# A state-space layer and a mixture of experts on one core: VectorE in chunk 0's lead, expert rows fetched in 32x32 blocks, squares per row tile

## The reference

```python
# part 1: a selective state space layer (512 inner channels, 16 states)
xn = rms_norm(ln(x)) * norm_w
x_inner, gate = split(xn @ in_proj_w)             # 256 -> 2 x 512
x_inner = x_inner * silu(gate)
xc = causal_conv(x_inner, conv_w)                 # 4 taps per channel
dt = softplus(xc @ dt_w + dt_b); Bm = xc @ B_w; Cm = xc @ C_w
h = exp(dt * A) * h + dt * Bm * xc                # along time, per channel and state
y = sum over states (h * Cm) + D_skip * xc
x = x + ln(y @ out_proj_w)
# part 2: 8 experts, the best 2 per row, and one shared expert
t = ln(x); logits = t @ gate_w; p, i = softmax of the top 2
x = x + ln(sum over the 2 (p * ((silu(t @ Wg[i]) * (t @ Wu[i])) @ Wd[i]))
           + (silu(t @ Sg) * (t @ Su)) @ Sd)
```

## Time and profile before

| what | value |
|---|---|
| median of 3 runs | 1672.4 us (1670.68 to 1673.68) |
| the profiled execution, its own time | 1672.79 us |
| its span | 1671.2 us |
| mean granted TensorE clock | 0.961 of full |
| PE busy | 1490.7 us, 89% |
| DVE busy | 1329.3 us, 80% |
| POOL busy | 1037.5 us, 62% |
| ACT busy | 1026.2 us, 61% |

### The profile page before, as it was taken

One profiled execution on the slowest core, in us unless ns is written; L12 is line 12 of the kernel. 1 busy time (PEld: TensorE's weight loads), 2 busy tenths in 40 slices (PEclk: granted clock), 3 DMA queues, 4 the chain that ended last, 5 costly groups with the idle time before them and its releaser, 6 DMA issues.

```text
span 1671.2 us, 23917 instructions
## 1 busy us (share of the span) xinstructions
PE 1490.7 (89%) x6642; PEld 991.6 (59%) x6642; DVE 1329.3 (80%) x2297; ACT 1026.2 (61%) x2140; POOL 1037.5 (62%) x1183
## 2 busy tenths in 40 slices
PE   6788799999999999999998677798999999999990
PEld 3354555655655655656656555476777777777760
DVE  4399999999999899999899994276666666676765
ACT  3567678679678678688686665254445454454544
POOL 0678779889889899899799884322222222323224
PEclk9999899999999999999999879799999999999995
DMA  6111112211221221211213734314222222222226
GB/s 205 39 51 39 51 57 67 85 58 40 88 63 46 73 62 54 80 52 55 67 52 114 221 104 158 130 27 133 33 36 36 36 36 36 36 36 36 36 32 206
DMA packets 88031, 119.90 MB, mean 72 GB/s; under 512 B 11168, under 2 KB 62208, under 8 KB 87904
## 3 DMA queue, kind: packets, MB, share of 16 engines
q1 hardware_dynamic: 66976, 86.61, 16.8%
q0 software_dynamic: 16704, 27.57, 8.4%
q10 hardware_dynamic: 4224, 4.19, 0.7%
HBM read 84.72 MB, written 33.10 MB: 71 GB/s over the span
## 4 chain that ended last, share of the span: by engine, by line
PE 40%; DVE 10%; POOL 9%; issue 9%; ACT 5%; DMA 1%; DVEq 0%; POOLq 0%; ACTq 0%; SPq 0%
PE A L1272 11%; PE bA L1241 10%; PE bH L1241 10%; POOL arena L1032 6%; DVE arena L870 5%; DVE arena_t L887 2%; PE bH L603 2%; PE A L484 1%; ACT bA L766 1%; PE A L566 1%; PE A L1263 1%; PE A L533 1%; DMA sum_scratch<-arena_t 1%; PE A L474 1%; POOL expert_in_scratch L1020 1%
## 5 line engine op out<-in xcount | busy, mean ns | idle before, releaser
L1032 POOL TENSOR_TENSOR arena<-arena 128x512 f32<-128x512 f32 x512 | 644.8, 1275 | 96.8 <-DVE arena L870 95.7
L766 ACT ACTIVATE bA<-arena,a_neg 128x512 f32<-128x512 f32 x512 | 350.5, 690 | 192.5 <-DVE arena L870 191.2
L603 PEld LDWEIGHTS bH<-ident,arena 128*128 128x128 f32 x2048 | 248.8, 145 | 285.1 <-issue 123.3
L603 PE MATMUL bH<-ident,arena 128*128 128x128 f32 x2048 | 324.7, 285 | 70.9 <-DVE arena L870 53.6
L870 DVE TENSOR_TENSOR_SCAN arena<-bA,arena 128x512 f32<-128x512 f32 x256 | 305.4, 1210 | 49.0 <-ACT bA L766 32.4
L870 DVE TENSOR_TENSOR_SCAN arena<-bA,hl,arena 128x512 f32<-128x512 f32 x256 | 321.2, 1270 | 2.5 <-ACT bA L766 2.1
L1305 ACT COPY hT<-arena_t 32x160 f32<-32x160 f32 x568 | 182.5, 321 | 77.0 <-DVE arena_t L1289 71.2
L1295 DVE STREAM_TRANSPOSE hT<-arena_t 32x192 f32<-32x192 f32 x568 | 206.1, 363 | 6.6
L1400 POOL DMA_INDIRECT sum_scratch<-arena_t x71 | 113.6, 1599 | 148.4 <-issue 120.7
L1272 PE MATMUL A<-arena,hT 128*128 x852 | 198.4, 383 | 2.1 <-DVE hT L1295 2.1
L1394 POOL DMA_DIRECT2D arena_t<-expert_in_scratch x71 | 40.8, 575 | 256.7 <-issue 256.7
(11 more groups left out here) (194 smaller groups left out, 2019.9 us busy)
## 6 DMA issues: line engine op xcount, KB each, us to landing
arena<-b_scratch SPq DMA_DIRECT2D x128, 256.0 KB, 3.2
arena_t<-expert_in_scratch POOLq DMA_DIRECT2D x71, 132.0 KB, 2.4
arena<-in_L_ffn_Wg_dram SPq DMA_DIRECT2D x8, 704.0 KB, 5.8
arena<-in_L_ffn_Wu_dram SPq DMA_DIRECT2D x8, 704.0 KB, 7.4
arena<-in_L_ffn_Wd_dram SPq DMA_DIRECT2D x8, 640.0 KB, 8.3
arena_x<-in_L_attn_x_dram SPq DMA_DIRECT2D x9, 512.0 KB, 5.0
arena<-in_L_attn_x_dram SPq DMA_DIRECT2D x8, 512.0 KB, 5.0
x_scratch<-arena_x SPq DMA_DIRECT2D x8, 512.0 KB, 3.2
```

The lines of the kernel that those rows point to most:

```text
L603: i = e.transpose(bH[g % NH][:, q * P:(q + 1) * P], hh[:, (n - 1) % 2, q, d * P:(d + 1) * P], ident[:])
L766: e.activation(bA[g % NA][:], dt[c % 2][:, d, :], ACT.Exp, scale=a_neg[:, d, n:n + 1]).then_inc(s_a, 1)
L1032: e.tensor_tensor(bb[:, k % NB, :], u[c % 2][:, d, :], br[:, n % NR, :], ALU.mult).then_inc(s_bb, 1)
```

## The change

It has three parts.

**Chunk 0's lead.** The convolutions of channel tiles 2 and 3 of chunk 0 are done by VectorE as one multiplication and three multiply-adds each (`dve_convs`), ahead of the 28 statistics. VectorE also takes chunk 0's softplus sums and input products (`step_sum`, `step_input`) from GpSimd and the norm of chunk 1's rows (`dve_norm_x`) from ScalarE. The first three scans, the first four decays and the first four GpSimd products stand inside the lead, between the `dt` steps of the channel tiles, instead of behind all of them.

**Expert rows.** SyncE fetches tile t (`sp_fetch`): eight DMAs, each moving four 32x32 blocks to where the other side of the diagonal is, and one for the 8 extra columns into a buffer of its own (`xm`, 8 deep). VectorE then transposes within 32x32 blocks (`dve_turn_in`), straight into `xtT`. TensorE's two transposes and ScalarE's copy go. A row buffer is free when its tile has been turned; the wait for the store stands only at `xm` and at the result scatter. The load of `x1` stands behind the fetch of tile 12.

**Squares.** Each square waits for its own addition, not for all four.

```diff
+FIRST = (2, 3)
+def by_hand(name, c):
+    return c == 0 and name in [f"cv{d}" for d in FIRST]
...
 def pe_lead(e, k, c):
-                e.wait_ge(s_xn, J * (c + 1))
                 room(e, b, c)
                 for j in range(J):
+                    e.wait_ge(s_xn, J * c + (J if c else j + 1))
...
@@ act_proj
                 e.activation(dt[par][:, m, :], dt[par][:, m, :], ACT.Ln, bias=1.0).then_inc(s_ln, 1)
+                if c == 0 and m:
+                    act_decay(e, 0, m - 1)
+                if c == 0 and m == ND - 1:
+                    act_decay(e, 0, m)
...
@@ act_post
-        if k == ACT_AT["square_xf"]:
-            e.wait_ge(s_x1, J * (c + 1))
-            for j in range(J):
-                i = e.activation(xf[:, j, 0:DM], xr[:, j, :], ACT.Square, bias=mv[:, c * J + j, 0:1], accum_out=sqx[:, j:j + 1])
-            i.then_inc(s_cl, 1)
+        for j in range(J):
+            if k == ACT_AT["square_xf"][j]:
+                e.wait_ge(s_x1, J * c + j + 1)
+                e.activation(xf[:, j, 0:DM], xr[:, j, :], ACT.Square, bias=mv[:, c * J + j, 0:1], accum_out=sqx[:, j:j + 1]).then_inc(s_cl, 1)
...
+    def dve_norm_x(e):
+        e.wait_ge(s_p0n, 2)
+        e.wait_ge(s_x, 32)
+        all_filled(e, ["xnT0", "xnT1"], 0)
+        for j in range(J):
+            i = e.tensor_scalar(xn[:, j, :], xp[:, j, :], r0[:, J + j:J + j + 1], nmr[:, J + j:J + j + 1], ALU.mult, ALU.add)
+        i.then_inc(s_xn, J)
+
+    def dve_convs(e):
+        for d in FIRST:
+            emptied(e, f"inner{d}", 0)
+        for q in range(TAPS):
+            for i, d in enumerate(FIRST):
+                to, tap = xc[0][:, d, :], w_cv[:, d, q:q + 1]
+                if q == 0:
+                    e.tensor_scalar(to, xin[:, d, 0:CH], tap, None, ALU.mult).then_inc(s_cv, 1)
+                else:
+                    e.wait_ge(s_cv, len(FIRST) * (q - 1) + i + 1)
+                    e.scalar_tensor_tensor(out=to, in0=xin[:, d, q:q + CH], scalar=tap, in1=to, op0=ALU.mult, op1=ALU.add).then_inc(s_cv, 1)
...
@@ dve_scans
-                if (loop, k) == (-1, 26):
+                if (loop, k) == (-1, max(DVE_AT["inner"])):
+                    dve_convs(e)
                     dve_stats_x(e, 1)
+                for m in range(ND):
+                    if (loop, k) == (-1, POOL_AT["dt"][m]):
+                        step_sum(e, 0, m)
+                        step_input(e, 0, m)
+                        if m == 0:
+                            dve_norm_x(e)
+                        else:
+                            dve_scan(e, 0, m - 1)
...
+    def sp_fetch(e, t):
+        if t >= NX:
+            e.wait_ge(s_kx, t + 1 - NX)
+        row = e.value_load(tab[0:1, 1, t:t + 1], min_val=0, max_val=SPARE + (E - 1) * P)
+        for q in range(P // BLK):
+            for k in range(KD):
+                e.dma_start(xt[q * BLK:(q + 1) * BLK, t % NX, k * P:(k + 1) * P].rearrange("j (a i) -> j a i", i=BLK),
+                            xs_d[bass.ds(row, P), k * P + q * BLK:k * P + (q + 1) * BLK].rearrange("(a j) i -> j a i", j=BLK)).then_inc(s_in[t % NX], 16)
+        if t >= NM:
+            e.wait_ge(s_gt, t + 1 - NM)
+            e.wait_ge(s_ys, 16 * (t + 1 - NM))
+        e.dma_start(xm[:, t % NM, :], xs_d[bass.ds(row, P), DM:RW]).then_inc(s_in[t % NX], 16)
...
+    def dve_turn_in(e, t):
+        fetched(e, t)
+        if t >= 2:
+            e.wait_ge(s_gu, t - 1)
+        e.transpose(xtT[:, t % 2, :, :].rearrange("p k q -> p (k q)"), xt[:, t % NX, :]).then_inc(s_kx, 1)
...
@@ sync_tiles
+        for t in range(NT):
+            sp_fetch(e, t)
+            if t == E + NX:
+                e.wait_ge(s_x1s, 16 * NCH)
+                for u in range(NU):
+                    e.dma_start(x1s[:, u, :, :], unit_rows(x1_d, u)).then_inc(s_x1u, 16)
...
@@ pool_tiles
+        for t in range(NT):
+            fetched(e, t)
+            e.wait_ge(s_yt, t + 1)
+            if t:
+                e.wait_ge(s_ys, 16 * t)
+            e.indirect_dma_start(out=sh_d, out_offset=bass.IndirectOffsetOnAxis(ap=xm[:].bitcast(U32)[:, t % NM, TOK - DM:TOK - DM + 1], axis=0),
+                                 in_=yt[:, t % 2, :], in_offset=None, compute_op=ALU.add).then_inc(s_ys, 16)
...
@@ pe_tiles
-            if t + 1 < NT:
-                pe_turn_in(e, t + 1)
...
@@ dve_tiles
+            if t + 1 < NT:
+                dve_turn_in(e, t + 1)
```

More of the change, by code:

```diff
@@ L83, in bank_table @@
             for names, c, now in ((POST, loop - 2, SLOTS + k), (PROJ, loop + 1, k), (POST, loop - 1, k), (LEAD, loop + 2, k)):
-                turn += [(name, c) for name in names if 0 <= c < NCH and slot(names, name, c) == now]
+                turn += [(name, c) for name in names if 0 <= c < NCH and slot(names, name, c) == now and not by_hand(name, c)]
     return {use: (i % NQ, i // NQ + 1) for i, use in enumerate(turn)}
@@ L186, in program @@
     take = places(arena_t)
-    xt = take(NX, RW)
+    xt = take(NX, DM)
     xtT = take(2, KD, P)
@@ L191, in program @@
     yt = take(2, DM)
[L192 removed]
+    xm = take(NM, RW - DM)
+    ge, gn = (arena_t[:, o:o + (NT + 1) * E].rearrange("p (t e) -> p t e", e=E) for o in (NX * DM + 2 * KD * P, NX * DM + 2 * KD * P + (NT + 1) * E))
     arena_x = sb("arena_x", [P, NU * UT * DM])
@@ L343, in program, with convs_filled, convs_emptied @@
     GATES, INNERS, CONVS = ([f"{name}{d}" for d in range(ND)] for name in ("gate", "inner", "cv"))
+    def convs_filled(e, c):
+        all_filled(e, [name for name in CONVS if not by_hand(name, c)], c)
+        e.wait_ge(s_cv, TAPS * len(FIRST))
+    def convs_emptied(e, c):
+        all_emptied(e, [name for name in CONVS if not by_hand(name, c)], c)
+        e.wait_ge(s_cv, TAPS * len(FIRST))
     def sh(c):
@@ L478, in pe_proj @@
             for q in range(TAPS):
-                if k == PROJ[b] + THIRD[q]:
+                if k == PROJ[b] + THIRD[q] and not by_hand(b, c):
                     if q == 0:
@@ L632, in act_lead @@
         for j in range(J):
-            if k == ACT_AT["norm_x"][j]:
+            if k == ACT_AT["norm_x"][j] and c != 1:
                 if j == 0:
@@ L658, in act_proj @@
         for d in range(ND):
-            if k == ACT_AT["conv"][d]:
+            if k == ACT_AT["conv"][d] and not by_hand(f"cv{d}", c):
                 filled(e, f"cv{d}", c)
@@ L1102, in pool_scan @@
         for loop in range(-2, NCH + 2):
-            if loop == 0:
-                e.wait_ge(s_cst, 5)
-                for k in range(AHEAD_POOL):
-                    pool_input(e, 0, k)
             for k in range(SLOTS):
@@ L1132, in act_scan @@
                 e.wait_ge(s_an, 2)
-            if loop == 0:
-                for k in range(AHEAD_ACT):
-                    act_decay(e, 0, k)
             for k in range(SLOTS):
@@ L1192, in dve_scans @@
             for k in range(SLOTS):
-                if 0 <= loop < NCH:
+                if 0 <= loop < NCH and (loop, k) not in [(0, d) for d in range(ND - 1)]:
                     dve_scan(e, loop, k)
@@ L1256, in pe_up @@
         pe_inner(e, ex, t, KD * FI, bU, s_gu)
-    def pe_turn_in(e, t):
-        e.wait_ge(s_in[t % NX], 16 * (t // NX + 1))
-        if t:
-            e.wait_ge(s_kx, t)
-        for k in range(KD):
-            i = e.transpose(bX[:, k * P:(k + 1) * P], xt[:, t % NX, k * P:(k + 1) * P], ident[:])
-        i.then_inc(s_tx, 1)
     def pe_down(e, t, ex):
@@ L1427, in act_tiles @@
     def act_tiles(e):
-        for t in range(-1, NT + 1):
+        for t in range(NT + 1):
             if t >= 1:
                 act_place(e, t - 1)
-            if 0 <= t < NT:
+            if t < NT:
                 e.wait_ge(s_g, t + 1)
```

119 lines of the change are left out of this document (54 added, 65 removed).

## The result

The changed kernel takes 1647.9 us (median of 4 runs, 1647.27 to 1648.47) against 1671.5 for the kernel before on the same chip (4 runs): a ratio of 0.9858, 95% interval 0.9846 to 0.987, faster by 1.4%. The forecast was 1643.5 with a range of 1633 to 1658. The profiled execution took 1647.27 us with a span of 1645.5, 25.7 less than the span before.

What follows compares the result with a forecast made beforehand. TensorE was taken to bound the expert tiles (7.55 us each), VectorE the scans, so the lead counts fully. From 1672.8: -15 tiles, -7.4 x1, +0.9 start, -1.4 squares, -6 lead gives 1643.9, as median 1643.5; range 1633 to 1658.

Steps and rivals of the forecast that it cites:

- Tiles' steady state (-15): Expert tiles: TensorE loses 0.22 us of transposes in each of 71 tiles, period 7.33 us; 15 us saved.
- x1 (-7.4): Load of x1 during the expert tiles: no fetch waits for a store there; 7.4 of 7.9 lost us regained.
- Squares (-1.4): Tail after the last scan: the last square starts right behind the last addition; 1.4 us saved.
- The start (+0.9): First expert tile: nine DMAs and the turn make the first gate product 1.3 us later; net 0.9 us lost.
- The lead (-6): Chunk 0 ahead of the scans: work moved to VectorE starts scans earlier; 6 us saved, bounds 2 to 9.
- By my list of the waits the fourth scan starts at 67.5: Chunk 0's lead: fourth scan at 67.5 us instead of 75.6.
- the cost that the prediction names against its own figure: Chunk 0's lead: TensorE idles some 4.5 us, then half speed over two `dt` tiles; up to 3.5 us lost.
- The first: Rival, expert tiles: SyncE's fetches set the pace; 1755 us at 8.9 us per tile; chance 0.09.
- the second: Rival: tiles gain, but the stall at x1 returns and the lead gives 2 us, not 6; 1655 us; chance 0.17.
- The third: Rival, expert tiles: late rows use up VectorE's slack and the period stays 7.55 us; 1659 us; chance 0.07.
- Its lower end, 1633: Whole kernel: 1633 us if the lead gives 9, the start costs nothing and SyncE is never felt.

Runs made afterwards that it cites:

- e7: Changed kernel with token tiles fetched in whole rows and turned by TensorE again, fetches still ahead of the stores; 1660.49 us, ratio 0.9934.
- e8: Changed kernel with one wait put back: SyncE fetches a tile only once the store of four tiles earlier has landed; 1735.84 us, ratio 1.0388.
- e3: Kernel before with only the squares changed, each waiting for its own addition; 1671.07 us, ratio 0.9993.
- e9: Changed kernel with the first token tile alone fetched in whole rows and turned by TensorE; 1645.8 us, ratio 0.9834.
- e2: Kernel before with only the lead part of the change, without TensorE's waits per row tile; 1671.62 us, ratio 0.9993.
- e5: Changed kernel with ScalarE's two statistics roots moved behind the softplus of dt tile 0; 1640.92 us, ratio 0.982.
- e1: Kernel before with one edit: in chunk 0 TensorE's transposes of normed rows wait for each row tile, not all four; 1671.65 us, ratio 1.0.
- e11: Changed kernel with each block fetch cut in two, 17 DMAs a tile; 1824.94 us, ratio 1.0908.

## Why the prediction held, and where it was off

The time lies in the range, 4.4 us above the forecast. The two large terms, for the tiles and for x1, are right in size and in mechanism. The lead was wrong in mechanism behind its fourth scan, and a head start that I had not forecast hid about half of that miss. Step by step:

- **Tiles' steady state (-15).** Right: 69 periods give 15.2, and e7, with a period of 7.55 again, takes them back. SyncE's 4.7 to 6.0 us are 5.1, VectorE's slack 1.45 for 1.4.
- **x1 (-7.4).** Right: 7.6. The reason given, that no fetch waits for a store any more, is borne out by e7, where the stall is gone without the blocks. Whether the stall would also have gone with the load's new place alone was not tried. What I had not seen is e8: the freed fetch is a condition of the whole gain, not only of these 7.6 us.
- **Squares (-1.4).** Right by the rows of e3 (1.5). Its time agrees (1.6 by the medians) but can't be told from zero.
- **The start (+0.9).** Mis-sized: +2.4 in this profile, and from +1.2 to +4.5 in the five kernels that start this way. Its 0.9 was 1.9 at the first gate product, and the slow product behind TensorE's 4.8 us wait was left out. e9 took 3.3 us out of that stretch (1087.74 - 1068.15 = 19.6 from the last scatter to the first down product, 22.9 in the changed kernel). The last down product's lower clock (+1.7) wasn't in the sum either.
- **The lead (-6).** Mis-sized, and the largest miss. The last scan moved by 4.2 us within the whole change, but 2.7 of these stand at VectorE's first multiplication, ahead of all that the term counts. Behind that point the lead gained 2.0 us to the sixth scan (1.5 in e2, and 1.0 by e2's median). So it was in part luck that "By my list of the waits the fourth scan starts at 67.5" came true at 67.73: the list puts it 67.5 - 28.9 = 38.6 us behind the first multiplication, and it came 41.5 behind it. These 3 us fit the cost that the prediction names against its own figure, up to 3.5 us for TensorE's idle time ahead of `dt` (4.0 us) and slow products behind it, of which it counted only 1.5. e5 removes that cost together with the delay of `bT`'s copy and gains 6 to 7 us. What failed outright is that I took the scans behind the fourth to follow without a gap. The sixth waits 3.0 us for a decay held up by TensorE's slow gate products, which moved by 4.3 us and not by 7.5. `pe_lead`'s wait for each row tile had no term in the sum; e1 can't tell it from nothing, and its share of the 2.7 us is open. (Six multiply-adds and two multiplications at the pitch given come to 4.5 us and not 4.7; they took 4.8.)
- **Rivals.** The first needed 0.76 us a DMA and found 0.5; e11 shows that with nearly twice the DMAs it decides. The stall's return, in the second, did not happen, but its 2 us for the lead is what the lead's own part gave. The third's late rows don't occur: VectorE's wait is for TensorE.
- **The range.** Its lower end, 1633, is not what its own terms give: a lead of 9 in place of 6 and a start of 0 in place of 0.9 make 1643.5 - 3 - 0.9 = 1639.6.

## What to carry to other kernels

When a fetch is cut into many small DMAs, count the DMAs first: here each cost its queue 0.5 us, with 64 pieces as with 128, so that nine fitted under the tile's 7.3 us and seventeen did not. Before such a cut, follow each wait ahead of the fetch around its loop (store, fetch, turn, scaling): one like it had delayed TensorE only around the load of x1 in the kernel before, and cost 88 us with the new fetch and turn. When a term seems confirmed by a time on the profile's clock, count it from an event just ahead of the edit as well: here 2.7 us of the lead's 4.2 stood there before VectorE had done any of its new work. And when a lead is shortened, look for the entry in another engine's list that waits longest for something not needed by what stands behind it: two roots at the wrong place cost 6 to 7 us, three times the 2.0 that the work moved to VectorE had brought.

## What the runs showed that I had not expected

- The issue of a DMA with 64 pieces costs SyncE what one with 128 does: 0.317 us, one start every 0.5.
- Waits of TensorE of 4.8, 4.3, 4.0 and even 2.1 us (4.79, 4.34 and 3.99 in the changed kernel; 2.08 ahead of its last product) were followed by slow products. The last product waits 2.07 to 2.18 us in all the kernels. It takes 2.85 us in seven of them (before, e1, e2, e3, e8, e9, e11) and 4.1 to 4.5 in the other seven: what decides it is not shown.
- Kernels with the same code up to the tiles reach the last scatter at times 2.8 us apart in their profiles. VectorE's first multiplication starts at 26.2 to 28.0 us in them already. The runs of one kernel differ by 1.2 us (the changed one) up to 8.9 (e8), so part of it is from run to run, and none of it is put down to a cause here.
